# Reordering the feed-forward chains of a fused two-layer block, and packing its experts into fifteen steps

## The reference

```python
x = x + L0_xattn(layernorm(x), ctx, mask0)      # 2 heads of 64
x = x + L0_ffn(layernorm(x))                    # sigmoid(xr Wr) * (relu(xk Wk)^2 Wv), xr and xk mixed with the token before
x = x + L1_xattn(layernorm(x), ctx, ctx, mask1) # 16 heads of 8, scores / sqrt(8), masked with -1e9
x = x + L1_ffn(layernorm(x))                    # 8 experts, inner width 352, silu(g) * u, each token to its best expert
```

## Time and profile before

| | |
|---|---|
| device time, median of 3 runs | 285.16 us (283.06 to 285.94) |
| profiled execution, device time | 284.44 us |
| its span | 282.6 us, so 1.84 us lie around it |
| busy: PE, DVE, ACT, POOL | 244.5, 190.4, 165.2, 96.5 us |
| mean granted clock of TensorE | 0.964 of 2.4 GHz |
| stages | first to 84.7 us, second to 223.8 us, experts to 282.6 us |

### The profile page before, as it was taken

The page is one execution under the profiler, slowest core; times in us unless marked ns, Lnnn a source line. Parts: engine busy times, 40 slices in busy tenths (PEclk is TensorE's granted clock), DMA queues, the critical chain, the costliest instruction groups (busy, mean ns, idle before and its releaser), DMA issues.

```text
span 282.6 us, 5562 instructions
## 1 busy us (share of the span) xinstructions
PE 244.5 (86%) x1866; PEld 136.0 (48%) x1883; DVE 190.4 (67%) x672; ACT 165.2 (58%) x304; POOL 96.5 (34%) x114
## 2 busy tenths in 40 slices
PE   0789999776897999999999998999978779999991
PEld 0344657554554345445544444454435325666651
DVE  3192674798899686779788878789686306676440
ACT  1157574635127478787888887878858514444440
POOL 2550856136201553012440042313122541455534
PEclk9999999999599599999999999999999979999997
DMA  6991174604562019999610999121000496016300
GB/s 187 399 428 60 59 130 133 172 10 142 98 163 87 2 44 304 299 282 227 183 46 29 251 361 376 44 49 52 21 0 2 125 342 269 28 47 191 104 12 9
DMA packets 20379, 40.77 MB, mean 144 GB/s; under 512 B 1502, under 2 KB 16484, under 8 KB 19392
## 3 DMA queue, kind: packets, MB, share of 16 engines
q1 hardware_dynamic: 9280, 27.52, 30.5%
q10 hardware_dynamic: 9792, 10.26, 13.8%
q0 software_dynamic: 1280, 2.64, 2.9%
HBM read 26.74 MB, written 14.20 MB: 145 GB/s over the span
## 4 chain that ended last, share of the span: by engine, by line
PE 43%; DVE 13%; ACT 5%; issue 4%; DMA 2%; POOL 1%; SPq 1%; POOLq 0%; DVEq 0%; ACTq 0%
PE banks L1441 9%; DVE scores_unused L1099 8%; PE banks L1494 6%; PE banks L1354 6%; PE banks L1427 5%; PE banks L1537 4%; PE banks L1422 3%; PE banks L1219 2%; ACT p_region L792 2%; PE banks L1526 2%; ACT banks L802 2%; DMA q_region<-binned_dram 1%; DMA binned_dram<-token_rows,mask_bias 1%; PE banks L1514 1%; PE banks L1517 1%
## 5 line engine op out<-in xcount | busy, mean ns | idle before, releaser
L1099 DVE CUSTOM_DVE_ANT_0 scores_unused<-banks,mask_bias 128x512 bf16<-128x512 f32 x128 | 82.6, 688 | 17.1 <-PE banks L1354 16.0
L792 ACT ACTIVATE p_region<-banks 128x1024 f32<-128x1024 f32 x64 | 65.3, 1021 | 30.7 <-PE banks L1427 30.2
L1354 PE MATMUL banks<-k_region,q_region 80*128 80x512 bf16 x128 | 44.0, 406 | 9.0 <-DVE max L1099 5.6
L1427 PE MATMUL banks<-q_region,k_region 80*128 80x256 bf16 x256 | 39.4, 277 | 0.3 <-ACT banks L802 0.3
L643 POOL COPY q_region<-q_region 8x768 bf16<-8x768 bf16 x16 | 13.0, 814 | 70.5 <-ACT q_region L776 70.5
L1441 PE MATMUL banks<-p_region,values 128*9 128x256 f32 x512 | 35.8, 402 | 0.0
L1427 PEld LDWEIGHTS banks<-q_region,k_region 80*128 80x128 bf16 x256 | 25.0, 99 | 15.8 <-issue 1.8
L802 ACT ACTIVATE banks<-mask_bias_by_key 128x1024 f32<-128x1024 bf16 x31 | 31.8, 1025 | 0.8
L549 POOL TENSOR_TENSOR ln_rstd<-ln_var_eps,minus_half 128x2 f32<-128x2 f32 x16 | 11.8, 736 | 54.9 <-DVE ln_var_eps L887 54.8
L1354 PEld LDWEIGHTS banks<-k_region,q_region 80*128 80x128 bf16 x128 | 11.3, 101 | 29.9 <-DVE max L1099 17.1
L1494 PE MATMUL banks<-k_region,q_region 128*64 128x352 f32 (+1 forms) x64 | 22.0, 463 | 0.6 <-ACT q_region L816 0.5
(11 more groups left out here) (157 smaller groups left out, 452.8 us busy)
## 6 DMA issues: line engine op xcount, KB each, us to landing
binned_dram<-ctx_region ACTq DMA_DIRECT2D x1, 7067.5 KB, 41.3
k_region<-experts_dram SPq DMA_DIRECT2D x9, 544.0 KB, 5.5
k_region<-k_parts_dram SPq DMA_DIRECT2D x4, 1152.0 KB
k_region<-experts_dram SPq DMA_DIRECT2D x1, 3808.0 KB, 18.4
binned_dram<-ctx_region ACTq DMA_DIRECT2D x1, 2441.5 KB, 24.7
q_region<-q_parts_dram SPq DMA_DIRECT2D x12, 192.0 KB
k_region<-mask1k_dram SPq DMA_DIRECT2D x1, 2048.0 KB, 12.7
k_region<-mask_dram SPq DMA_DIRECT2D x1, 2048.0 KB, 17.0
```

The costliest lines, as they stand in the source:

```text
L792: a.activation(pt[:, u % 2, j, :, :].rearrange("p (c t) q -> p c (t q)", c=2), ps[:, c:c + 2, :], ACT.Exp, scale=float(D1) ** -0.5).then_i ...
L1099: return v.tensor_tensor_reduce(out=junk[:, q, :], in0=scores, in1=m1b[:, QT * (u // 4) + q, :], scale=1.0, scalar=-3e38, op0=ALU.add, op1 ...
L1354: return m.matmul(out, qst[0:R, (u * GH + j) * SQ + q * P:(u * GH + j) * SQ + (q + 1) * P], kst[0:R, (u * GH + j) * SK:(u * GH + j + 1) * ...
L1427: last = m.matmul(ps[:, first + c, t * SQ:(t + 1) * SQ], kst[0:R, k:k + P], qst[0:R, (u * GH + j) * SQ:(u * GH + j + 1) * SQ], start=False ...
```

## The change

- **Feed-forward chains, batches 0 and 1.** `rr`, `vv` and `s3` of a batch now share one slot (9 for batch 0, 13 for batch 1), `n3` and `l3T` the next (10, 14), `Q` 11 and 16, `parts` 11 and 16. The squares `k2` leave DVE: ACT does a `Square` right behind its relu in `kk`, for all four batches. `QS` begins in slot 14 with two, then 4, 4, 2, instead of slot 15 with 4, 4, 4.
- **Masks of batches 2 and 3.** `c1k` 2, `c1` 2, `c1k` 3 and `c1` 3 leave slots 12 and 13 for parts (0, 3), (1, 2), (2, 2), (2, 3) of the second attention; `fm` 2 leaves slot 16 for part (2, 0). SP puts keys 2 back only behind keys 3 out.
- **Experts.** The two phases share a step (step 9: the eleventh further half of phase 0, and expert 0 of phase 1), and phase 1 has three further halves. Sixteen steps become fifteen, `gin` shrinks with them, and six weight loads of 544 KB remain of eight, each with a buffer of its own. Rows of the fixed steps come by 6 DMAs in phase 0 (those of step 1 first) and 3 in phase 1.
- **End of the attention.** `weigh(15)` comes first, then `turn_h(0)`, `turn_rows(1)`; ACT follows with `copy_out(15)` first.

```diff
-PHASE_STEPS = tuple(FIXED + n for n in MORE)
-PHASE_AT = (0, PHASE_STEPS[0])
-STEPS = sum(PHASE_STEPS)
+HALVES = [(0, True, e) for e in range(E)] + [(0, False, n) for n in range(2 * MORE[0] - 1)]
+HALVES += [(1, True, e) for e in range(E - 1)] + [(1, False, 0), (1, True, E - 1)] + [(1, False, n) for n in range(1, 2 * MORE[1] - 1)]
+STEP_HALVES = list(zip(HALVES[0::2], HALVES[1::2]))
+STEPS = len(STEP_HALVES)
+MIXED = FIXED + MORE[0] - 1
+PICKED = range(MIXED, MIXED + FIXED)
...
-EARLY_AT = {"Q": 13, "parts": 13, "n0": -7, "q": -5, "k0_": -5, "PV": 5, "kk": 9, "wo": 6, "s2": 6, "n2": 7, "fm": 8, "l2T": 8}
-LATE_AT = {"k2": 9, "V": 4, "l3T": 12, "s0": -8, "rr": 9, "lnT": -6, "v0_": 1, "vv": 11, "s3": 11, "K": 3}
+EARLY_AT = {"n0": -7, "q": -5, "k0_": -5, "PV": 5, "kk": 9, "wo": 6, "s2": 6, "n2": 7, "l2T": 8}
+LATE_AT = {"V": 4, "s0": -8, "lnT": -6, "v0_": 1, "K": 3}
...
-EARLY0 = beside0(EARLY_AT, {2: [("mix", 0)], 12: [("n3", 0)]})
-LATE0 = beside0(LATE_AT, {5: [("c1k", 0)], 7: [("c1", 0)], 9: [("c1k", 1)], 10: [("c1", 1)], 12: [("c1", 2)], 13: [("c1k", 2), ("c1k", 3), ("c1", 3)]})
-FIRST_Q = {15: (0, 4), 16: (4, 8), 17: (8, 12)}
+EARLY0 = beside0(EARLY_AT, {2: [("mix", 0)], 8: [("fm", 0)], 10: [("n3", 0)], 11: [("Q", 0)], 12: [("fm", 1)], 14: [("n3", 1)], 16: [("Q", 1)]})
+LATE0 = beside0(LATE_AT, {5: [("c1k", 0)], 7: [("c1", 0)], 9: [("c1k", 1), ("rr", 0), ("vv", 0), ("s3", 0)], 10: [("l3T", 0), ("c1", 1)],
+                          11: [("parts", 0)], 13: [("rr", 1), ("vv", 1), ("s3", 1)], 14: [("l3T", 1)], 16: [("parts", 1)], 17: [("rr", 2)]})
+FIRST_Q = {14: (0, 2), 15: (2, 6), 16: (6, 10), 17: (10, 12)}
...
-    (0, 0): [("wo", 3)], (0, 1): [("s2", 3)], (0, 2): [("vv", 2)],
-    (1, 0): [("s3", 2), ("n2", 3)], (1, 1): [("n3", 2)], (1, 2): [("l3T", 2)], (1, 3): [("l2T", 3)],
-    (2, 1): [("Q", 2)], (2, 2): [("rr", 3)],
+    (0, 0): [("wo", 3)], (0, 1): [("s2", 3)], (0, 2): [("vv", 2)], (0, 3): [("c1k", 2)],
+    (1, 0): [("s3", 2), ("n2", 3)], (1, 1): [("n3", 2)], (1, 2): [("l3T", 2), ("c1", 2)], (1, 3): [("l2T", 3)],
+    (2, 0): [("fm", 2)], (2, 1): [("Q", 2)], (2, 2): [("rr", 3), ("c1k", 3)], (2, 3): [("c1", 3)],
...
-    (4, 0): [("k2", 3)], (4, 1): [("fm", 3)], (4, 2): [("vv", 3)],
+    (4, 1): [("fm", 3)], (4, 2): [("vv", 3)],
...
-ROWS_IN_AT = {0: (9,), 9: (14,), 10: (15,)}
+ROWS_IN_AT = {0: (9,), 8: (13, 14)}
...
             keys_out(2)
-            sp.wait_ge(m1_conv, B)
-            keys_back(2)
 
             arrived(sp, f"PV{B - 1}")
             query_rows(1)
             queries_out(1)
+            query_rows(2)
             keys_out(3)
-            query_rows(2)
+            sp.wait_ge(m1_conv, B)
+            keys_back(2)
             queries_out(2)
...
+                if ph == 0:
+                    for ks in (range(1, 2), range(2, FIXED), range(1)):
+                        for r in range(2):
+                            load(r, r, ks, ks[0], 0 if ks[0] == 1 else 1)
+                else:
+                    load(0, 1, range(FIXED), MIXED, 1)
+                    load(1, 0, range(FIXED - 1), MIXED + 1, 1)
+                    load(1, 1, range(FIXED - 1, FIXED), MIXED + FIXED, 1)
...
                     emptied(a.activation(kact, half(job), ACT.Relu), job)
+                    copied(act, job)
+                    a.activation(kact, kact, ACT.Square).then_inc(kact_done, 1)
...
-                if kind == "k2":
-                    copied(dve, f"kk{b}")
-                    v.tensor_tensor(kact, kact, kact, ALU.mult).then_inc(kact_done, 1)
...
+            copy_out(UNITS - 1)
+            turned_h(0)
             turned_rows(1)
-            turned_h(0)
-            copy_out(UNITS - 1)
             pipeline(step, 0)
...
+                elif n in PICKED:
+                    first = HALF if n == MIXED else 0
+                    if n == MIXED:
+                        pe.wait_ge(more_in[table_column(n)], 16)
+                        m.transpose(out[:, 0:HALF], gin[0:HALF, n, 0:D], ident[0:HALF, 0:HALF])
                     pe.wait_ge(picked_set, QT)
...
-            pe.wait_ge(exp1, UNITS * GH - 1)
-            turn_rows(1)
-            turn_h(0)
             weigh(UNITS - 1, 0)
             weigh(UNITS - 1, 1)
+            turn_h(0)
+            turn_rows(1)
             pipeline(step, 0)
```

More of the change, by code:

```diff
@@ L44 @@
 EXPERT = 2 * I + 3 * D
-STAGES = 7
 STAGES_SOONER = 3
@@ L150, in phase_of, with further, table_column @@
     return 0 if b in PHASE_BATCHES[0] else 1
[L153 to L162 removed]
+def further(s):
+    return [r for r in range(2) if not STEP_HALVES[s][r][1]]
+def table_column(s):
+    r = further(s)[0]
+    ph, _, n = STEP_HALVES[s][r]
+    return MORE_AT[ph] + (n + ph) // 2
+STAGED = [s for s in range(STEPS) if 1 in further(s)]
 def scores_at(u):
@@ L511, in whose @@
-                _, r = nc.values_load_multi_w_load_instructions(experts[ph][:, n:2 * n], engines=[sp.engine], min_val=0, max_val=E - 1,
+                first = 1 if ph else MORE[ph]
+                steps = [s for s in STAGED if STEP_HALVES[s][1][0] == ph]
+                _, r = nc.values_load_multi_w_load_instructions(experts[ph][:, first:first + len(steps)], engines=[sp.engine], min_val=0,
+                                                                max_val=E - 1,
                                                                 skip_runtime_bounds_check_because="the table is clamped to it")
-                for k in range(n):
-                    second[at + k] = r[k]
@@ L534, in _ @@
             whose(1)
-            for d in range(MORE_AT[1], sum(MORE)):
-                weights_in(d)
+            for s in STAGED[-1:]:
+                weights_in(s)
             for r in range(YBUFS):
```

106 lines of the change are left out of this document (52 added, 54 removed).

## The result

The median went from 284.48 us (283.06 to 285.94, four runs) to **276.07 us** (273.00 to 276.94, four runs), a ratio of 0.9685 with an interval of 0.9590 to 0.9779. The forecast was 275.8 us. The profiled execution took 273.00 us, the fastest of the four, its span 270.3 us (before: 284.44 and 282.6).

What follows compares the result with a forecast made beforehand. PE was taken as full in expert steps and nearly so in the second attention; the first stage's end was held by batch 0's chain, DVE and a slow clock. -5.0 + 1.3 - 3.1 - 2.6 = -9.4 us gave 275.8 us, range 271.0 to 281.0.

Steps and rivals of the forecast that it cites:

- Part 1: First stage, chain of batch 0: `parts` 0 ends 4.3 us sooner, and PE's 2.88 us wait for queries goes.
- Part 2: DVE in the first stage: less work, last early maximum ends at 80.5 instead of 85.5 us; with Part 1, -5.0 us.
- 6.4 us out of a DVE that was the fuller engine in front of the early maxima: First stage: four conversions (4.39 us), three squares (1.6) and `fm` 2 (about 0.4) leave DVE.
- the price that I set against the rule: Feed-forward squares: 0.38 us each on ACT, like a relu, costed at nothing, against 0.523 us on DVE.
- Part 3: Second attention: takes over four conversions and `fm` 2, +1.3 us, bounds 0 and +4.5.
- all of its 0.7 us shows: Second attention, part (2, 3): the conversion `c1` 3 holds PE up by its full 0.7 us.
- `c1` 2 near POOL: Second attention: conversion `c1` 2 runs near POOL's split of the last keys and may show half.
- The slower rival: Second attention: keys 2 and queries 2 wait in the blank fill, batch 2 comes late, 290.3 us; chance 0.05.
- Queries 2 home some 10 us before: Second attention: queries 2 return some 10 us before PE wants batch 2 at 144.25 us; costed at nothing.
- Part 4: End of the attention: last unit weighed first, `gate_up(1)` starts 3.1 us sooner, bounds -1.5 and -3.6.
- Part 5: Expert steps: fifteen instead of sixteen where PE is full, -2.6 us, lower bound 0.
- the clock stays up: Rival: clock at its upper level through the first stage's end and units 0 and 1, 272.8 us; chance 0.13.

Runs made afterwards that it cites:

- first pair: The first profiles of the kernel before and of the changed kernel, compared stretch by stretch; profiled executions of 284.44 and 273.00 us.
- f3: Changed kernel with the four mask conversions of batches 2 and 3 back in slots 12 and 13 of the first attention: 287.08 us, ratio 1.0088.
- g3: Changed kernel with the four squares back on VectorE and SP's expert weight loads issued only behind the last unit: 276.44 us, ratio 0.9739.
- second pair: The kernel before (282.66 us) and the changed kernel (275.28 us), both run again and profiled on one chip, that of group g.
- f4: Changed kernel with step 1's rows turned before the last unit is weighed, as in the kernel before: 285.41 us, ratio 1.0054.
- g4: Changed kernel with GpSimd's row gathers spread over expert steps 0 to 4: 274.35 us, ratio 0.9691.
- g2: Changed kernel unaltered, run again on the chip of group g: 275.28 us, ratio 0.9693.
- f1: Changed kernel unaltered, run again on the chip of group f: 288.52 us against 285.96 us of the kernel before, ratio 1.0165.
- e2: Kernel before with only the fifteen steps and their six smaller row loads, step 1's first; old order at unit 15: 288.82 us, ratio 1.0187.
- the chip of f: Chip of the second group of runs, all on the changed kernel or variants of it; unaltered it took 288.52 us there.
- e3: Kernel before with only the last unit weighed first, on PE and ACT, row loads as they were: 292.05 us, ratio 1.0349.
- the chips of e and f: Chips of two groups of four runs: e, parts of the change on the kernel before; f, the changed kernel (288.52 us) and variants.
- e1: Kernel before with parts 1 to 3 alone (chain order, squares on ACT, moved masks, SP's and POOL's lists): 284.82 us against 288.1, ratio 0.9995.
- f2: Changed kernel with SP writing the queries of batch 2 before it brings back keys 2: 286.98 us, ratio 1.0094.

## Why the prediction was right, and where not

**Part 1: right.** From `rr` 0 to the end of `parts` 0 took 62.50 - 46.46 = 16.04 us before and 55.41 - 43.66 = 11.75 after, 4.3 us sooner as forecast. From there to the first early score it took 65.18 - 55.41 = 9.8 us (9.1 forecast); PE came to it behind a wait of 1.33 us for DVE's norm of batch 1, not for the trip through DRAM, so the wait for `q_parts_dram` went.

**Part 2: the size right, the cause wrong.** The first stage gained 4.67 and 4.84 us (5.0 forecast). In the first pair 3.60 us of it lie between `rr` 0 and the first early score (25.12 us before, 21.52 after) and 1.07 us behind it, where the kernel before had 6.8 us at half speed and the changed one none. How much of the 1.07 us is clock no run tells; the forecast had put nothing on it. Neither the conversions (f3: 32.34 us with them) nor the squares of batches 0 and 1 (g3: 32.51) had a share; each was put back alone, not both together. The step that failed is "6.4 us out of a DVE that was the fuller engine in front of the early maxima": the chains' order makes the gain, and VectorE gets waits of 3.10 and 3.78 us for PE in which that work is free. I had counted busy time and not looked for where the new order would leave it idle. The rule of the Trainium skill's page "ScalarE: Activation LUTs" (Rules for kernel authors) and my reading of the rows against it differ by 0.35 us at most here (g3), against the rule and less than a run can show in its time, and the price that I set against the rule was off: the square takes 0.416 us on ACT, not the relu's 0.382, and 0.422 on VectorE in g3 beside 0.523 in the earlier trace rows. No table was loaded for it; the trace of the changed kernel has one ACT_TABLE_LOAD, at 1.69 us.

**Part 3: its items mostly off.** Forecast +1.3. The second pair has +1.72: 0.64 is unit 2, and 1.1 lie in units 0 and 1, which had 10.2 instead of 6.8 us at half speed. The first pair has -0.45, below the lower bound of 0: unit 1 fell by 2.22 us, since its 6.8 us at half speed went, unit 2 grew by 1.15, and unit 6 by 0.78 for the wait for the queries below. Unit 3, where I had "all of its 0.7 us shows", did not grow (9.59 us in both). `c1` 2 near POOL cost more: the conversions of the changed kernel's profile, against the earlier trace rows:

```profile
86.32 1.10 DVE L973 TENSOR_SCALAR mask_bias_by_key<-k_region 128x1024 bf16<-128x1024 int32 x1
92.75 1.15 DVE L969 TENSOR_SCALAR mask_bias<-k_region 128x1024 bf16<-128x1024 int32 x1
...
102.66 0.69 DVE L973 TENSOR_SCALAR mask_bias_by_key<-k_region 128x1024 bf16<-128x1024 int32 x1
```

The fourth took 0.69 us too, so two of four met POOL. There unit 2 took 9.65 us, and so it did in f4 and g4, whose first two conversions took 1.10 to 1.16 us; in g2 and f1, where none or only one met it slightly (0.81 us, in unit 1), 9.15.

**The slower rival was nearer than its 0.05.** "Queries 2 home some 10 us before" failed: in the first profile their write took 16.7 us (108.39 to 125.08), and PE waited:

```profile
136.52 0.59 PE L1376 MATMUL banks<-k_region,q_region 80*128 80x512 bf16 x2 [0.62 <-DMA q_region<-q_parts_dram]
```

PE wants the first scores of batch 2 at 136 us, not 140.5: with the early start and a full clock the attention came to them sooner while the fill of the bins took 48.4 us (41.3 in the earlier trace rows). In the other two profiles of the changed kernel, f1 and g2, PE had no such wait. Earlier work also calls earlier for what comes by DMA; I had not moved that need far enough forward.

**Part 4: the size right where no signal was late, the credit too narrow.** Forecast -3.1, measured -3.38 and -3.91. The step that failed is that the last unit has to be weighed first to earn it: f4 and e2 reach the second `gate_up` in 4.26 and 4.25 us with the rows turned first, 0.4 us less than the 4.66 of the changed kernel. There the load of step 1's rows as the first and smallest of six, which came with part 5, cuts the wait to 0.55 to 0.60 us, and weighing first adds nothing to it; on the chip of f it costs 3.1 us in the medians (288.52 against 285.41). Yet e3 has the order without the load, and its PE turned step 1's rows 4.07 us behind unit 14's output with the weighing done. In g2 `gate_up(1)` follows that turning by 1.02 us, so without the late signal e3 would have come to it after some 5.1 us, 2.9 less than before (an estimate from these two traces). Either edit removes the wait, and the forecast counted them as one.

**Part 5: right.** -2.58 and -2.45 us for one step (2.6 forecast).

**The sum.** That the stretches of the first pair come to -9.5 us beside a forecast of -9.4 is in part luck: part 3 and unit 15 together have +1.13 against +1.3, but as -0.45 and +1.58, both of them mostly the clock's. The 0.7 us between the profiled execution and the median was not borne out either: it was 0.04 us with four runs before, and 3.1 after.

**Clock.** The rival "the clock stays up" came true in the first profile (270.3 us of span, clock 0.992), in part in the other runs there (0.971 to 0.980). That a kernel with fewer waits can also lose more to the clock, as f1 does, was not among the rivals: there PE's idle time came from signals that no view of before had shown late. The forecast of 275.8 us holds on the two sittings whose profiles show none (276.07 and 275.28) and misses on the third (288.52).

**Open.** Why PE's signals come late on two chips. In f1 GpSimd had issued six gathers in a row until 227.44 us, and SP's three weight loads took 2.75 us to issue, 1.40 in g2; at the second place four indirect DMAs stood in a row. That is coincidence in time and no more: g2 has the same series of gathers, and the two kernels built to tell the causes apart (g3, g4) ran where no signal was late. The recording, whose events got lost at the same time, is a rival that nothing here tests. Nor was the kernel before profiled on the chips of e and f; that e1 stands for its end is an inference from the same code. A version with f4's order and g4's gathers is what the runs point to; it wasn't built, and g4's 274.35 us, while the lowest median, can't be told from g2's.

## What to carry to other kernels

Read what a chain order does from where it leaves each engine waiting, not from busy time alone: work that moves into such a wait is free, and moving it elsewhere earns nothing. Where two edits could each remove the same wait, undo each of them once before either is given the credit. And a gain near a tight hand-over between engines (here PE to ScalarE, 0.04 us on one chip and 4.5 on another) is to be measured on more than one chip, since there the clock turned 3.9 us saved into 4.7 lost.

## What the runs showed of the hardware that I had not expected

- The signals of finished TensorE instructions came 3.6 to 4.6 us after the recorded end at unit 15 and 1.5 to 3.0 us near the ninth expert step, several at once, in all eight profiles of two chips (in e1's at the second place alone), and in none of a third. In the profile it reads as an idle time of the waiting engine that ends by "remote". In the same eight over a third of the landing events behind 210 us are missing.
- SP's issue of three 544 KB loads took 1.40 us in g2 and 2.75 us in f1, in the same stretch.
- A write of 192 KB behind a blank fill of 7 MB took 8.1 us in the kernel before (116.38 to 124.48), 10.2 us in f2, and 15.2 to 16.7 us with the 1.15 MB of keys 2 ahead of it as well (the changed kernel, f1, g2).
- Two samples of one program on one chip gave 282.66 (four runs) and 283.89 us (seven runs), 0.4% apart; the ratio of 0.9852 comes from two of the four. A difference of 1.5% between two kernels in one sitting needs its stretches read before it is believed.
